# A Mamba block and a mixture of experts on one core: Delta summed in DRAM by accumulating DMAs

## What is computed

```python
z = x @ W_in
val, gate = jnp.split(z, 2, axis=-1)
val = silu(conv3(val))
B_proj = val @ W_B
C_proj = val @ W_C
combined_delta = val @ W_delta + delta_base
Delta = jax.nn.softplus(combined_delta @ W_tau)
A = -jnp.exp(A_log)
dA = Delta[..., None] * A
A_bar = jnp.exp(dA)
B_bar = jnp.expm1(dA) / (dA + 1e-06) * Delta[..., None] * B_proj[:, :, None, :]
# h = A_bar * h + B_bar * val;  y = sum(h * C_proj) over 16 states, for each token in turn
out = y * silu(gate) @ W_out + residual
```

## Time and profile before

| | us |
|---|---|
| median of 3 runs | 5096.31 |
| lowest and highest run | 5090.79, 5102.79 |
| the profiled execution, its own time | 5096.16 |
| its span, from the first to the last instruction | 5094.4 |
| mean granted TensorE clock | 0.869 |

### The profile page before, as it was taken

The page is one execution under the profiler, slowest core; times in us unless marked ns, Lnnn a source line. Parts: engine busy times, 40 slices in busy tenths (PEclk is TensorE's granted clock), DMA queues, the critical chain, the costliest instruction groups (busy, mean ns, idle before and its releaser), DMA issues.

```text
span 5094.4 us, 36516 instructions
## 1 busy us (share of the span) xinstructions
PE 3923.5 (77%) x9708; PEld 1628.3 (32%) x9708; DVE 4214.9 (83%) x3766; ACT 4024.4 (79%) x4251; POOL 3723.2 (73%) x2228
## 2 busy tenths in 40 slices
PE   6551232888898888888888888888888876868989
PEld 3210110333333333333333333333333323333443
DVE  1278799999999999999999999999998999999110
ACT  2486788889899898889899888899998988977111
POOL 0188887787888887778888787787788897878101
PEclk8775565899999999999999999898999997979999
DMA  4388876777786877777777878787777777777322
GB/s 136 126 266 244 245 203 196 208 223 225 215 250 193 258 208 227 207 224 220 216 234 219 244 196 251 196 235 207 225 224 213 228 217 196 219 198 216 97 99 75
DMA packets 343640, 1053.92 MB, mean 207 GB/s; under 512 B 40965, under 2 KB 43909, under 8 KB 336134
## 3 DMA queue, kind: packets, MB, share of 16 engines
q1 hardware_dynamic: 274314, 799.91, 45.8%
q0 software_dynamic: 69120, 251.69, 25.8%
HBM read 673.29 MB, written 126.51 MB: 157 GB/s over the span
## 4 chain that ended last, share of the span: by engine, by line
ACT 22%; issue 19%; POOL 17%; PE 17%; DMA 12%; DVE 11%; SPq 0%; POOLq 0%; DVEq 0%; ACTq 0%
DMA ysum<-hs 10%; POOL inv L1316 5%; PE ps L1038 5%; ACT inv L684 4%; POOL hs L1295 4%; PE ps L1054 4%; PE ps L1008 4%; ACT inv L679 3%; DVE ps L1092 2%; DVE ps L1099 2%; ACT th L691 2%; DVE ps L1086 2%; POOL ysum L1303 2%; ACT inv L689 2%; ACT abar L694 2%
## 5 line engine op out<-in xcount | busy, mean ns | idle before, releaser
L1316 POOL TENSOR_TENSOR inv<-inv,th 128x1024 f32<-128x1024 f32 x512 | 1271.8, 2484 | 259.2 <-ACT th L691 256.3
L1295 POOL TENSOR_TENSOR hs<-hs,Cb 128x1024 f32<-128x1024 f32 x480 | 1209.9, 2521 | 63.1 <-DVE hs L1119 42.9
L1038 PE MATMUL ps<-hf,w1r 128*128 128x512 f32 x2304 | 1133.0, 645 | 65.5 <-DMA w1r<-in_W 38.8
L1065 PE MATMUL ps<-Brow,pick 48*128 48x512 bf16 x1024 | 356.9, 433 | 805.9 <-DVE hs L1119 803.0
L1054 PE MATMUL ps<-w2r,hid 128*128 128x512 f32 x1792 | 842.1, 618 | 13.3 <-issue 13.3
L691 ACT ACTIVATE th<-delta,halfA 128x1024 f32<-128x1024 f32 x512 | 583.3, 1139 | 310.6 <-POOL inv L1316 310.5
L1086 DVE TENSOR_TENSOR ps<-ps,us 128x1024 f32<-128x1024 f32 x512 | 628.1, 1227 | 107.3 <-PE ps L1065 106.7
L1303 POOL DMA_DIRECT2D ysum<-hs x480 | 444.5, 926 | 336.9 <-DMA ysum<-hs 324.0
L1099 DVE SCALAR_TENSOR_TENSOR ps<-ps,coef,inv 128x1024 f32<-128x1024 f32 x512 | 658.6, 1286 | 31.9 <-POOL inv L1316 7.4
L1038 PEld LDWEIGHTS ps<-hf,w1r 128*128 128x128 f32 x2304 | 460.9, 207 | 664.4 <-issue 611.6
L1106 DVE SCALAR_TENSOR_TENSOR ps<-nrd,inv_kappa,ps 128x1024 f32<-128x1024 f32 x512 | 659.1, 1287 | 15.0
(11 more groups left out here) (157 smaller groups left out, 5237.9 us busy)
## 6 DMA issues: line engine op xcount, KB each, us to landing
Cb<-c_rows SPq DMA_DIRECT2D x512, 512.0 KB, 4.6
ysum<-hs POOLq DMA_DIRECT2D x480, 512.0 KB, 5.4
w2r<-w_scaled SPq DMA_DIRECT2D x144, 512.0 KB, 7.1
w1r<-in_W SPq DMA_DIRECT2D x144, 512.0 KB, 4.7
gbc<-expert_gates SPq DMA_DIRECT2D x128, 256.0 KB, 5.0
aw<-in_W_val SPq DMA_DIRECT2D x64, 256.0 KB, 5.1
xa<-in_x SPq DMA_DIRECT2D x32, 512.0 KB, 6.4
h_residual<-hT SPq DMA_DIRECT2D x16, 1024.0 KB, 7.5
```

Of the source, the lines that this page charges most:

```text
L1038: mm = t.matmul(o, w1r[:, n % 2, k, h * P:(h + 1) * P], hf[:, k, :], start=(k == 0), stop=(k == G - 1))
L1295: gp_.tensor_tensor(hs[:, c % 3, :] if c % N else ysum[:], hs[:, c % 3, :], Cb[:, c % 2, :], ALU.mult).then_inc(hC_done, 1)
L1316: gp_.tensor_tensor(inv[:, c % 6, :], inv[:, c % 6, :], th[:, c % 2, :], ALU.mult).then_inc(thinv_done, 1)
```

## The change

Delta is no longer summed in SBUF. relu(p) is stored to DRAM by SyncE in slots 14 and 15; GpSimd then adds the correction (its sign turned: e minus the rounded value is now kept in tt1) by an accumulating DMA from SBUF to DRAM in slots 15 and 16, and ln(1 + e) by another in slots 17 and 20. Each waits for the landing of the one before it. GpSimd's log1p subtraction and VectorE's addition are gone, and their semaphores. VectorE takes p from PSUM in slots 9, 10 and 11, adding the bias and applying the upper bound in one instruction; ScalarE's four evictions are gone. The loads of Delta and of the next x wait for the landing of the log's DMAs; the load for the next unit pair moves from slot 18 to 19.

```diff
@@ semaphores
-        a_abs, a_exp, a_relu, a_t, a_corr, a_ln, a_log1p, delta_done = (
-            sem("a_abs"), sem("a_exp"), sem("a_relu"), sem("a_rounded"), sem("a_correction"), sem("a_ln"), sem("a_log1p"),
-            sem("delta_done"))
...
+        a_abs, a_exp, a_relu, a_t, a_corr, a_ln = (
+            sem("a_abs"), sem("a_exp"), sem("a_relu"), sem("a_rounded"), sem("a_correction"), sem("a_ln"))
+        st_delta, st_corr = [sem("relu_stored_0"), sem("relu_stored_1")], [sem("correction_added_0"), sem("correction_added_1")]
+        st_ln = [sem("log_added_0"), sem("log_added_1")]
...
@@ sync_slot
-                if g == 0:
-                    sp.wait_ge(st_delta, 64 * k + 48)
-                if g == 2:
-                    sp.wait_ge(st_delta, 64 * (k + 1))
+                if g % 2 == 0:
+                    sp.wait_ge(st_ln[g // 2], 32 * (k + 1))
...
-            if r == 18 and H % 2 and 0 <= (H + 1) // 2 < NK:
-                load_unit(G * ((H + 1) // 2))
...
-            if r in (17, 21) and has(qa):
-                gp = r // 21
-                sp.wait_ge(delta_done, 2 * qa + gp + 1)
-                store_half(delta_d, qa, 2 * gp, 2 * gp + 2, pre[:, 2 * gp:2 * gp + 2, :]).then_inc(st_delta, 16)
+            if r in (14, 15) and has(qa):
+                gp = r - 14
+                sp.wait_ge(a_relu, 2 * qa + gp + 1)
+                store_half(delta_d, qa, 2 * gp, 2 * gp + 2, pre[:, 2 * gp:2 * gp + 2, :]).then_inc(st_delta[gp], 16)
...
+            if r == 19 and H % 2 and 0 <= (H + 1) // 2 < NK:
+                load_unit(G * ((H + 1) // 2))
             if r in (19, 21) and has(qn):
                 part = r // 21
-                ge(sp, delta_done, 2 * qn - 1 + part)
+                ge(sp, st_ln[part], 16 * qn)
...
@@ act_window
-                    ge(act, st_delta, 32 * q)
+                    ge(act, st_delta[0], 16 * q)
+                    ge(act, st_delta[1], 16 * q)
...
-                    ge(act, a_log1p, 2 * q)
+                    ge(act, st_corr[0], 16 * q)
+                    ge(act, st_corr[1], 16 * q)
...
-            def take_p(q, gs):
-                if has(q):
-                    act.wait_ge(st_h, 16 * (q + 1))
-                    for g in gs:
-                        act.wait_ge(mm_p, G * q + g + 1)
-                        s.activation(pre[:, g, :], ps[:, bank_of["p", q, g], :], ACT.Identity,
-                                     bias=tau_bias[:, g:g + 1]).then_inc(ev_p, 1)
...
-                    if place == 0:
-                        take_p(qa, (0, 1))
-                    if place == 1:
-                        take_p(qa, (2, 3))
@@ dve_slot
-            def softplus(q, gp):
-                if has(q):
-                    part = slice(2 * gp, 2 * gp + 2)
-                    dve.wait_ge(a_log1p, 2 * q + gp + 1)
-                    dve.wait_ge(a_relu, 2 * q + gp + 1)
-                    v.scalar_tensor_tensor(pre[:, part, :], pre[:, part, :], DELTA_HI, lnw[:, part, :], ALU.min, ALU.add).then_inc(delta_done, 1)
+            def take_p(q, g):
+                if has(q):
+                    dve.wait_ge(st_h, 16 * (q + 1))
+                    dve.wait_ge(mm_p, G * q + g + 1)
+                    v.tensor_scalar(pre[:, g, :], ps[:, bank_of["p", q, g], :], tau_bias[:, g:g + 1], DELTA_HI, ALU.add,
+                                    ALU.min).then_inc(ev_p, 1)
...
+                if r in (9, 10):
+                    take_p(qa, r - 9)
+                if r == 11:
+                    take_p(qa, 2)
+                    take_p(qa, 3)
...
-                if r in (16, 20):
-                    softplus(qa, r // 20)
@@ pool_slot
-                    gp_.tensor_tensor(tt1[:, part, :], tt1[:, part, :], lnw[:, part, :], ALU.subtract).then_inc(a_corr, 1)
-
-            def log1p(q, gp):
-                if has(q):
-                    part = slice(2 * gp, 2 * gp + 2)
+                    gp_.tensor_tensor(tt1[:, part, :], lnw[:, part, :], tt1[:, part, :], ALU.subtract).then_inc(a_corr, 1)
+
+            def delta_rows(q, gp):
+                return delta_d[q // 2, 2 * gp:2 * gp + 2, :, (q % 2) * T:(q % 2 + 1) * T].rearrange("g p t -> p g t")
+
+            def add_correction(q, gp):
+                if has(q):
+                    pool.wait_ge(a_corr, 2 * q + gp + 1)
+                    pool.wait_ge(st_delta[gp], 16 * (q + 1))
+                    gp_.dma_start(delta_rows(q, gp), tt1[:, 2 * gp:2 * gp + 2, :], accum_op=ALU.add).then_inc(st_corr[gp], 16)
+
+            def add_log(q, gp):
+                if has(q):
                     pool.wait_ge(a_ln, 2 * q + gp + 1)
-                    gp_.tensor_tensor(lnw[:, part, :], lnw[:, part, :], tt1[:, part, :], ALU.subtract).then_inc(a_log1p, 1)
+                    pool.wait_ge(st_corr[gp], 16 * (q + 1))
+                    gp_.dma_start(delta_rows(q, gp), lnw[:, 2 * gp:2 * gp + 2, :], accum_op=ALU.add).then_inc(st_ln[gp], 16)
...
-            if r in (16, 19):
-                log1p(qa, r // 19)
...
+            if r in (15, 16):
+                add_correction(qa, r - 15)
+            if r == 17:
+                add_log(qa, 0)
+            if r == 20:
+                add_log(qa, 1)
```

4 lines of the change are left out of this document (2 added, 2 removed).

## The result

The changed kernel took 5114.35 us, median of 7 runs (5109.57 to 5125.81); the kernel before, on the same chip, 5102.79 (7 runs). The ratio is 1.003 with a 95% interval of 1.0018 to 1.0042: slower by 0.3%, where the prediction said faster by 0.6%. 5114 lies above its range as well.

A forecast was written before the change was run, and what follows sets the result against it. No engine bounds the whole; the chain of waits through ScalarE, GpSimd and, in some windows, VectorE does. Per window 4.0 - 1.0 - 0.3 = 2.7 us, times 14 = 38; 5096.2 - 38 + 8 = 5066 us, range 5018 to 5110.

The forecast's parts named there:

- ScalarE: Four p evictions fewer on ScalarE: 2.3 us per window off the chain, its next tanh sooner by as much.
- VectorE's evictions: Slots 9 to 11: four evictions at 0.68 us, 2.7 us more per window; VectorE and what follows it move by +0.3.
- the prediction's signs: Expected trace signs, among them both p pairs and subtractions off the chain and new evictions at 0.67 to 0.69 us.
- GpSimd's issues: Slots 15, 16, 17, 20: four new DMA issues at 0.93 us each, two on the chain, 1.9 us, against 4.7 removed.
- The y sum's landing: Before gate_y: the 4.59 us wait was taken as there anyway, with slot 16's new issue hidden in it.
- Rival 3: Shared software queue delays the y sum before gate_y, landing 12.1 us for 5.4: slower, 5132 us; chance 0.16.
- The test that the prediction gave itself: Prediction wrong if the y sum's median landing rises above 7 us, among other limits.
- The lead at slot 21: GpSimd about 4.0 us ahead at slot 21: 1.6 past slot 18, plus 2.36 from the second subtraction gone.
- The x wait: Slot 22: VectorE's statistics wait for the x load behind the log's landing, 0 to 2.4 us, taken as 1.0.
- Before the first state: Two accumulates in a row delay the second chunk's x load and the first delta load: 8 us more together.
- Sum: All terms: 38 us less over 14 windows, 8 us more before the first state, giving 5066 us.
- rival 1: The whole of the chain's work is gained: 5.2 us per window, 73 in 14 windows, 5025 us; chance 0.18.

The follow-up runs named there:

- e1: The kernel before with only the four p evictions of a chunk moved to VectorE, in slots 9 to 11: 5090 us, ratio 0.9980.
- e8: The changed kernel with every accumulating DMA into Delta cut to 16 of 512 columns, issues, waits and order kept: 5057 us, ratio 0.9906.
- e17: The changed kernel with its four accumulating DMAs of a chunk turned into plain stores to spare DRAM rows, still issued by GpSimd: 5063 us, ratio 0.9924.
- e15: The changed kernel without the second half's correction DMA; the first half's in slot 15 and both log DMAs stay: 5113 us, ratio 1.0024.
- e3: The changed kernel without the two correction DMAs of a chunk; the log's DMA waits for relu's store instead: 5077 us, ratio 0.9951.
- e4: The changed kernel without any accumulating DMA into Delta; correction and log are computed but left out: 5026 us, ratio 0.9849.
- e13: The kernel before with p evictions on VectorE and GpSimd's first log1p subtraction moved behind the issue of gate_y's y sum in slot 16: 5089 us, ratio 0.9977.

## Why the prediction was wrong, step by step

**ScalarE, right.** The tanh of state 16 came 2.1 us sooner after slot 13's start (2.3 forecast), and the wait before the rounding step is gone from slot 13.

**VectorE's evictions, right in the main.** 0.743 us, without spread (739 to 751 ns), where 0.68 was taken: 0.25 us per window. The rule on shared ports that the prediction cited (the Trainium skill, page "SBUF — State Buffer", section "Who interferes with whom") agrees with that missing spread. TensorE's transposes, costed at nothing, waited 58.2 us in 12 windows for the last eviction; slots 0 to 12 are 0.8 us longer, in e1 0.6. Why e1 brought 10 us and not 21 stays open: in its profile, an execution 7 us under the median, the window is 1.4 us shorter, where 1.5 was expected. What follows VectorE was to come 0.3 us later; it enters slot 14 1.1 us sooner, since only 0.8 of the evictions' time shows at slot 13. Off the chain the evictions are not, as the prediction's signs wanted: they are on it in six windows.

**GpSimd's issues, mis-sized.** Taken at 0.93 us, the lower end of 0.93 to 1.85; measured 1.53 and 1.20. Four cost 5.5 us per window, the two subtractions that went had cost 4.7. The argument for the lower end, that the bytes are the same, failed: e8 moves 1/32 of the bytes for the same issue time. As a plain store the same tiles take 1.01 and 0.76 us (e17), in about half the packets. Also, in 3 of windows 1 to 13 the second correction had to wait 4.4 to 5.1 us for relu's store, and in a fourth (window 7) 6.2 us that the trace gives to no releaser; the prediction gave it "a slot or more".

**The y sum's landing: the step that failed first.** The prediction took the landing before gate_y as unchanged and hid an issue in it. Rival 3 named the mechanism and was put at 0.16, since "the correction is issued a slot, some 8 us, before that y sum". But the correction lands after 8.8 us, so it is still under way when the y sum is issued, 6.2 us later in window 7 of e15 (2399.8 and 2406.0). Nor did the prediction ask what an accumulate into DRAM costs beyond its bytes, which e17 shows to be the larger part. The landing rose from 5.5 to 8.2 us, not to the 12.1 of rival 3; some 0.7 of that is there with no correction either (6.1 to 6.3 in e3, e4 and e13). It was enough, since the gain which it had to eat at that place was 2.8 and not 5.2: in windows 1 to 13 the y sum of state 15 was issued 2.8 us sooner after slot 13's start, and gate_y stood 2.7 us longer behind it. The test that the prediction gave itself, a median landing above 7 us, was the wrong one: the median of all 480 went from 5.4 to 5.8 us only, as most of the harm sits in one y sum of the thirty of a window (the y sum of state 18, behind the first log, went from 7.0 to 8.3).

**The lead at slot 21, wrong in size.** 4.0 us forecast for GpSimd, with the y sum of state 19 issued so much sooner. Measured, on the mean of windows 1 to 13 and from the window's start: 0.1 us sooner (1.5 in e3, 2.5 in e4). gate_y came as late as before (46.0 us after slot 13's start, 46.1 before), and GpSimd's weights then made VectorE wait in slots 18 and 19 (1.5 and 0.7 us longer). VectorE does enter slot 21 3.8 us ahead, as L1154 is gone from slot 20, but that lead is hollow: it waits there for a y sum, and slot 21 is 2.0 us longer in e4 too, with no accumulate at all. The prediction had no term for that wait.

**The x wait, mechanism right, size wrong.** The log's landing of 7.6 us is inside 5.4 to 9.1; the wait was 30.5 us in 14 windows, 2.2 each, where 1.0 of 0 to 2.4 was taken. It ate what lead was left, and by e3 and e4 the logs cost the states 35 of the 53 us, the corrections 18. The estimate of 3.2 us that the prediction drew from the Trainium skill, page "DMA: Bandwidth & Descriptors", section "Anatomy of one DMA — SWDGE (gpsimd) path", found no support here: no accumulate of 512 KB into DRAM landed under 5.8 us, and even 16 KB took 2.7 to 8.1 (e8).

**Before the first state, right in sum, by luck in its parts.** 8.7 us for 8 forecast. The second chunk's x load came 7.7 us later (153.1 and 160.8) for 4.5 to 6.5 forecast, and the first delta load 8.6 later (236.8 and 245.5), so its own part is 1.0 for 2.2 to 4.2.

**Sum.** In place of -38 + 8 it was +1 in the states, +8.7 in front and +6.7 behind, the last not the change's. Had every term come as hoped, e4's 4379 says, the states would have given 52 us, less than rival 1's 73. ScalarE's tanh of state 20 may be the reason: in e4 GpSimd took it up 0.1 us after its end in 6 of windows 1 to 13 (4 before). No run tests that.

## What to carry to other kernels

In this kernel, summing in DRAM was not a store with the addition for free: an accumulate took about twice a plain store's engine time and one and a half to two us more of landing, and its issue half a us more, perhaps for its packets. So price it from a run of its own, and then look which DMA is issued next, who waits for its landing, and who waits for the accumulate itself. Look at the one landing that is on the chain, not at the median of its line. And part of a change may be the best of it: half of Delta in DRAM, its correction behind the last y sum before gate_y and its log in slot 25, together with the evictions' move and one log1p in gate_y's wait gained 0.9%, where all of Delta in DRAM lost 0.3%.
